# A Trainium2 kernel in detail: the query and key stacks of an eight-wide self attention laid out by DMAs, one per head, in place of 0/1 products and copies from PSUM

## The reference, cut to what matters

```python
q, k, v = x @ Wq, x @ Wk, x @ Wv              # layer 3 also: biases and rotary embedding
q, k, v = (t.reshape(B, T, 16, 8).transpose(0, 2, 1, 3) for t in (q, k, v))
scores = q @ k.swapaxes(-1, -2) / sqrt(8)      # layers 0 and 1: causal
ctx = softmax(scores) @ v                      # T = 512 queries and keys
```

## Time and profile before

| | |
|---|---|
| median of 3 runs | 3211.59 us (3202.09 to 3213.86) |
| profiled execution, its own time | 3200.05 us |
| span in the profile | 3198.3 us |
| PE busy | 2715.7 us (85%) |
| DVE busy | 1759.3 us (55%) |
| ACT busy | 1373.9 us (43%) |
| POOL busy | 602.8 us (19%) |
| mean granted PE clock | 0.87 of full speed |

### The profile page before, as it was taken

How to read it: one execution, slowest core, us unless ns; L and a number is a source line. 1 busy time by engine, 2 the same in 40 slices (tenths; PEclk the granted TensorE clock), 3 DMA queues, 4 the chain that set the end, 5 groups by cost and what they waited for, 6 DMA issues and landing times.

```text
span 3198.3 us, 41256 instructions
## 1 busy us (share of the span) xinstructions
PE 2715.7 (85%) x14161; PEld 1369.0 (43%) x14161; DVE 1759.3 (55%) x4863; ACT 1373.9 (43%) x3204; POOL 602.8 (19%) x849
## 2 busy tenths in 40 slices
PE   6898998889987888888879988987899788889885
PEld 3233335334543675244423333452345347732353
DVE  5535437645654687624565444476357548776154
ACT  2545622452324543564435556225532345335741
POOL 1220001220112672000013200003201138610000
PEclk9988998988878998869779888998898689988776
DMA  4000000000000000000100000000001000000000
GB/s 168 2 1 1 1 1 25 26 2 20 29 19 1 1 27 27 1 1 31 37 8 2 1 1 1 1 26 26 1 20 33 14 1 1 27 28 1 1 1 7
DMA packets 16432, 49.71 MB, mean 16 GB/s; under 512 B 1761, under 2 KB 8801, under 8 KB 14434
## 3 DMA queue, kind: packets, MB, share of 16 engines
q1 hardware_dynamic: 15650, 45.79, 4.1%
q10 hardware_dynamic: 576, 1.29, 0.1%
HBM read 45.43 MB, written 1.05 MB: 15 GB/s over the span
## 4 chain that ended last, share of the span: by engine, by line
PE 66%; DVE 17%; ACT 9%; issue 6%; POOL 1%; DMA 0%; SPq 0%; ACTq 0%; DVEq 0%; POOLq 0%
PE psum L582 5%; PE psum L2155 4%; PE psum L995 4%; PE psum L549 4%; PE psum L572 3%; PE psum L1006 3%; DVE floor_s L2254 2%; PE psum L979 2%; PE psum L1530 2%; PE psum L1822 2%; PE psum L1360 2%; PE psum L821 2%; PE psum L746 2%; ACT PT_s L648 2%; PE psum L1818 2%
## 5 line engine op out<-in xcount | busy, mean ns | idle before, releaser
L648 ACT ACTIVATE PT_s<-psum 128x512 f32<-128x512 f32 (+3 forms) x768 | 344.9, 497 | 277.7 <-PE psum L572 276.0
L396 POOL TENSOR_SCALAR ve<-mv 128x4 f32<-128x4 f32 x48 | 13.5, 281 | 1668.9 <-DVE mv L386 1668.7
L708 DVE CUSTOM_DVE_ANT_0 rest_s<-psum,packed_early 128x128 f32<-128x128 f32 (+3 forms) x512 | 226.6, 487 | 152.2 <-PE psum L555 150.1
L2181 POOL TENSOR_TENSOR buffer<-sim_s 128x1024 f32<-128x1024 f32 x128 | 271.7, 2138 | 171.7 <-DVE floor_s L2254 86.9
L572 PE MATMUL psum<-QS_s,KS_s 64*128 64x512 bf16 (+3 forms) x768 | 199.3, 364 | 36.1 <-DVE mx_s L708 16.6
L555 PE MATMUL psum<-KS_s,QS_s 64*128 64x512 bf16 (+3 forms) x768 | 186.9, 354 | 43.2 <-DVE mx_s L711 20.1
L582 PE MATMUL psum<-PT_s,vaug 128*9 128x512 f32 (+3 forms) x1536 | 179.4, 542 | 45.3 <-POOL PT_s L681 29.4
L681 POOL TENSOR_SCALAR_AFFINE_SELECT PT_s<-PT_s 128x128 f32<-128x128 f32 x512 | 146.0, 294 | 340.3 <-ACT PT_s L648 334.8
L711 DVE TENSOR_REDUCE mx_s<-psum 128x1 f32<-128x512 f32 x256 | 161.8, 683 | 83.7 <-PE psum L555 82.9
L1043 ACT ACTIVATE PT_s<-psum 128x512 f32<-128x512 f32 (+1 forms) x224 | 121.0, 592 | 164.4 <-PE psum L997 164.3
L2214 ACT ACTIVATE above_s<-buffer,below_s 128x1024 f32<-128x1024 f32 x128 | 145.2, 1149 | 96.6 <-POOL buffer L2181 58.0
(11 more groups left out here) (446 smaller groups left out, 5382.8 us busy)
## 6 DMA issues: line engine op xcount, KB each, us to landing
buffer<-packed_experts SPq DMA_DIRECT2D x36, 384.0 KB, 3.3
buffer<-packed_moe SPq DMA_DIRECT2D x4, 2048.0 KB, 8.2
buffer<-packed_cross SPq DMA_DIRECT2D x4, 2048.0 KB, 7.9
buffer<-packed_product SPq DMA_DIRECT2D x4, 1024.0 KB, 4.9
packed_early<-packed_early SPq DMA_DIRECT2D x1, 2654.5 KB
QS_s<-nmT_s SPq DMA_DIRECT2D x144, 4.0 KB
raw_s<-packed_setup SPq DMA_DIRECT2D x1, 1840.0 KB, 7.6
packed_late<-packed_late ACTq DMA_DIRECT2D x4, 314.0 KB, 3.7
```

Of the source, the lines that this page charges most:

```text
L648: a.activation(PT[:, u // 4 % 2, i, q0_of(c):T], bank[u % 3][:, q0_of(c):T], ACT.Exp, scale=scale).then_inc(exp_done.sem, 1)
L708: v.tensor_tensor_reduce(junk[:, u % 2, 0:w], bank[n % 4][:, 0:w], s.w["causal"][:, T - w:T], 1.0, -3e38, ALU.add, ALU.max, mx[:, j, h:h + ...
L2181: g.tensor_tensor(fs[:, n % 2], m[:, 0, :].unsqueeze(2).to_broadcast([P, NK, NK]), m[:, 1, :].unsqueeze(1).to_broadcast([P, NK, NK]), ALU. ...
```

## The change

`parts` now has six slots per operand, in the order of the stack, instead of three. `split_up` writes the three parts to their first slots (`FIRST_SLOT`), and four copies on ACT fill the slots in which a part stands again (`MORE_SLOTS`): for keys and queries each, part one to two more slots, then part two to one more. SP waits for both splits and all four copies and then issues 32 DMAs, one for each head's keys and one for its queries, pair by pair, each from 8 partitions by 6 slots of `parts` to 48 rows of `KS` or `QS`, 1 KB a row. They count on four semaphores (`PAIR_GROUPS`): pair 0; pair 1; pairs 2 and 3; pairs 4 to 7. Two more DMAs bring the rows of ones of `KS` from device memory. The ring holds scores and the one turn alone; before the first score of a group PE waits for the group's DMAs. The stack order within a head becomes row = 6 * d + slot for both operands. `selq`, `selk` and `maxrows` and their loads are gone. Products read the 48 rows (score) or 51 rows (`st`) of a head instead of 64.

```diff
+SLOTS = 6
+FIRST_SLOT = {"q": (0, 3, 5), "k": (0, 1, 2)}
+MORE_SLOTS = {"q": (slice(1, 3), slice(4, 5)), "k": (slice(3, 6, 2), slice(4, 5))}
+PAIR_GROUPS = ((0, 1), (1, 2), (2, 4), (4, 8))
...
-    for i in range(HEADS8 // 2 + 1):
-        if i < HEADS8 // 2:
-            ring += [("stack", 2 * i), ("stack", 2 * i + 1)]
-        if i >= 1:
-            ring += [("score", u) for u in range(2 * TJ * (i - 1), 2 * TJ * i)]
-        if i == HEADS8 // 4 + 1:
+    for i in range(HEADS8 // 2):
+        ring += [("score", u) for u in range(2 * TJ * i, 2 * TJ * (i + 1))]
+        if i == HEADS8 // 4:
             ring.append(("turn", 0))
...
-    parts = s.tile("parts", [P, 2, 3, T], BF16)
+    parts = s.tile("parts", [P, 2, SLOTS, T], BF16)
...
+    def stack(h, more=0):
+
+        return slice(64 * (h % 2), 64 * (h % 2) + SLOTS * HD8 + more)
...
-        pe.wait_ge(*keys_split(4))
-        pe.wait_ge(*queries_split(4))
         pe.wait_ge(*v_ready(1))
...
-            if kind == "stack":
-                i, q = u // 2, 1 - u % 2
-                sel = (s.w["selq"], s.w["selk"])[q]
-                for w in range(3):
-                    mm = pe.matmul(bank[n % 4][:], sel[:, w, i, :], parts[:, q, w, :], start=(w == 0), stop=(w == 2))
-                mm.then_inc(ring_ready.sem, 1)
-            elif kind == "score":
+            if kind == "score":
                 h, j = scores[u]
-                pe.wait_ge(*stacks_copied(2 * (h // 2) + 2))
+                for loaded, (first, last) in zip(pairs_loaded, PAIR_GROUPS):
+                    if u == 2 * TJ * first:
+                        pe.wait_ge(*loaded(64 * (last - first)))
...
     def sync(sp):
+        yield T1 - 2
+        for ready in (keys_split(4), queries_split(4), keys_repeated(2), queries_repeated(2)):
+            sp.wait_ge(*ready)
+        for loaded, (first, last) in zip(pairs_loaded, PAIR_GROUPS):
+            for h in range(2 * first, 2 * last):
+                for q, to in ((1, KS), (0, QS)):
+                    sp.dma_start(to[stack(h), h // 2, :], parts[h * HD8:(h + 1) * HD8, q, :, :]).then_inc(loaded.sem, 16)
+        for o in range(2):
+            row = 64 * o + SLOTS * HD8
+            sp.dma_start(KS[row:row + 3].rearrange("p i t -> p (i t)"), s.ones_rows).then_inc(ones_loaded.sem, 16)
...
+        for n in range(2):
+            for q, name, split, repeated in ((1, "k", keys_split, keys_repeated), (0, "q", queries_split, queries_repeated)):
+                yield T1 - 5 + 2 * n + 0.5 * (1 - q)
+                a.wait_ge(*split(2 * n + 1))
+                to = parts[:, q, MORE_SLOTS[name][n], :]
+                a.copy(to, parts[:, q, FIRST_SLOT[name][n]:FIRST_SLOT[name][n] + 1, :].to_broadcast(to.shape)).then_inc(repeated.sem, 1)
...
-            if kind == "copy":
-                i, q = u // 2, 1 - u % 2
-                n = slot[("stack", u)]
-                a.wait_ge(*ring_ready(counted[("stack", u)]))
-                if q == 1:
-                    a.activation(KS[:, i, :], bank[n % 4][:], ACT.Identity, bias=s.w["maxrows"][:, 0:1]).then_inc(stacks_copied.sem, 1)
-                else:
-                    a.copy(QS[:, i, :], bank[n % 4][:]).then_inc(stacks_copied.sem, 1)
```

More of the change, by code:

```diff
@@ L427, in attention8_plan @@
     ring = []
-    for i in range(HEADS8 // 2 + 1):
-        if i < HEADS8 // 2:
-            ring += [("stack", 2 * i), ("stack", 2 * i + 1)]
-        if i >= 1:
-            ring += [("score", u) for u in range(2 * TJ * (i - 1), 2 * TJ * i)]
-        if i == HEADS8 // 4 + 1:
+    for i in range(HEADS8 // 2):
+        ring += [("score", u) for u in range(2 * TJ * i, 2 * TJ * (i + 1))]
+        if i == HEADS8 // 4:
             ring.append(("turn", 0))
-    follow = {"stack": "copy", "score": "max", "turn": "rows"}
+    follow = {"score": "max", "turn": "rows"}
     for n, (kind, u) in enumerate(ring):
@@ L510, in freed @@
         kind, u = ring[n]
-        if kind == "turn":
-            return max_copied(u + 1)
-        return stacks_copied(u + 1) if kind == "stack" else scores_read(u + 1)
+        return max_copied(u + 1) if kind == "turn" else scores_read(u + 1)
     def tensor(pe):
@@ L657, in split_up @@
     def split_up(eng, q, done):
-        whole, left, part = qk[:, q, :], rest[:, q, :], parts[:, q, :, :]
-        eng.tensor_copy(part[:, 0, :], whole).then_inc(done.sem, 1)
+        whole, left = qk[:, q, :], rest[:, q, :]
+        first, second, third = (parts[:, q, n, :] for n in FIRST_SLOT["qk"[q]])
+        eng.tensor_copy(first, whole).then_inc(done.sem, 1)
         eng.wait_ge(*done(1))
-        eng.tensor_tensor(left, whole, part[:, 0, :], ALU.subtract).then_inc(done.sem, 1)
+        eng.tensor_tensor(left, whole, first, ALU.subtract).then_inc(done.sem, 1)
         yield
         eng.wait_ge(*done(2))
-        eng.tensor_copy(part[:, 1, :], left).then_inc(done.sem, 1)
+        eng.tensor_copy(second, left).then_inc(done.sem, 1)
         eng.wait_ge(*done(3))
-        eng.tensor_tensor(part[:, 2, :], left, part[:, 1, :], ALU.subtract).then_inc(done.sem, 1)
+        eng.tensor_tensor(third, left, second, ALU.subtract).then_inc(done.sem, 1)
     def gpsimd(g_):
```

40 lines of the change are left out of this document (15 added, 25 removed).

## The result

| | before | after |
|---|---|---|
| median | 3211.59 us of 5 (3199.47 to 3213.86) | 3167.63 us of 5 (3166.54 to 3194.17) |
| profiled execution, its own time | 3200.05 us | 3194.17 us |
| mean granted PE clock in the profile | 0.87 | 0.82 |

A forecast was written before the change was run, and what follows sets the result against it. PE was taken to bound the kernel, 66% of its chain. Credits of 113, 20 and 2 us less 12, 24, 4, 9, 4 and 6 made 76, plus 9 for the plan: gain 85, time 3120 us, range 3068 to 3188.

The forecast's parts named there:

- What the change takes away: 576 0/1 products on PE's chain in the rings, 113 us, and the stack copies on ACT, 20 us.
- what is late next: In the rings, DVE and its maxima, close behind PE, take back part of the gain: -9, -4 and -6 us.
- The copies, the plan and the setup: Stack copies gone from ACT, 20 us; shorter planned order, +9 us (-15 to +30); fewer setup loads, +2 us.
- (a): ACT's four new copies and its wait for the split: -12 us, bounds from +6 to -48.
- (b): PE's wait at T1 for split, ACT's last copy, four DMA issues and landing: -24 us, bounds -10 to -45.
- (c): Later pairs' DMAs land in time, barely, for their scores: -4 us, bounds 0 to -25.
- (d): SP's queue: 34 issues ahead of the same run's 12 spreads take 21 us; nothing late, cost 0.
- (e): DMA engines: a run's 1536 rows take 10 us over 8 engines, within SP's 20 us of issue.
- (f): Setup: DVE waited 2.17 us for the last load, of which 1.5 MB go: +2 us.
- The range: Bounds together: gain about 130 us with all good ends, about 20 with all bad; final range 3068 to 3188.
- Rival 2: Something else was as late: first waits, ACT's part and the DVE bound leave 15 to 40 us, 3165 to 3190; 16%.
- Rival 4: SP's issue costs more than 0.63 us: at 0.9 the gain is gone, at 1.1 3220 us or more; 10%.

The follow-up runs named there:

- direct: Changed kernel without its 32 pair DMAs a run; two ACT copies fill pair 0 and all heads read it: 3127.61 us, ratio 0.9747.
- filler6: direct with six idle products ahead of each pair's first score, 576 in all: 3172.31 us, ratio 0.9878.
- one_product: Kernel before, with one 0/1 product per stack instead of three, so 384 of 576 go: 3166.23 us, ratio 0.9859.
- before_wait: Kernel before, plus four DMAs of 24 rows after the split, for which PE waits ahead of its first stack: 3219.05 us, ratio 1.0038.
- direct_rest: Changed kernel with pair 0 filled by two ACT copies, pairs 1 to 7 by their 28 DMAs with all waits: 3136.93 us, ratio 0.9759.
- filler: direct with three idle products ahead of each pair's first score, 288 in all: 3139.57 us, ratio 0.9802.

## Why the prediction had the direction and missed the size

The forecast's direction rested on PE's chain and held. The failed step is the first part of "What the change takes away": 576 products, credited with their 113 us on the chain. Put back as idle products they were worth 42 to 45 us.

- **The products, 113 us.** Measured 45 us (direct to filler6; 42 by the ratios), and 44 for 384 of them in one_product. The forecast took 19 off for what is late next, so 94 stand against 45. The sum took each product's length on the chain as what its removal gives. It isn't: with the products gone the mean granted clock is 0.843 and not 0.871, and 56 us come back in the lengths of three groups of the remaining products (direct against filler6). I had the clock in the earlier trace rows, 0.93 and 0.89 in the two stretches, and asked only how long the products were, never whether the clock would stay.
- **The copies, the plan and the setup, less (a): 20 + 9 + 2 - 12 = 19 us.** From before (3209) to filler6 (3172), which differ in these, it is 37 us, so this side was under by 18. One thing in it the sum had no term for: filler6 reaches its first scores 27 us sooner in all than before (70 against 97), as two copies between tiles of SBUF stand there in place of twelve products and copies from PSUM. The rest can't be told apart further. ACT's four copies took 1048 ns and 624 ns, 39 us in all, where I had 42. ACT waited 33.3 us ahead of them, near the 48 of the bound, but there is no sign that PE stood behind it.
- **(b), 24 us.** 31 to 36, or 33 to 45 by the ratios, and that against direct, which itself has two copies between split and first score. My baseline was another, PE's first stack; for just that wait, in the old order, before_wait has 11 us. And measured to the first score the path became shorter by the change, 97 to 81 us in all, since twelve products and two copies had stood in it before. The first score came 5.3 to 5.8 us after the split in the first four runs and not 4.5: an issue each 0.72 us in place of 0.63, and 3.0 us from the last issue's start in place of 2.65. The wait and its length were right; what it costs at the end depends on the order around it, which the sum of shortfalls doesn't see.
- **(c) and (d), 4 us.** 4 to 9 us by the medians. Groups came late only at pairs 1, 2 and 4 of the first run of all (0.7, 2.9 and 6.0 us of idle), where no other stream's work stands between the scores. SP runs at 0.72 us an issue, 23 us for 32.
- **(e).** The 16 DMA engines were busy 0.40 of 610:650, and no group came late there.
- **(f).** The first split ended 3.0 us earlier than before (36.28 to 39.32): in line with the setup's 2 us.
- **What is late next, 19 us.** In part it came, and at DVE as I had it: PE's idle time ended by the maxima (L708, L711 and their like), over scores, stacks or idle products, and transposed scores, is 60 us in filler6 and 78 in direct. From filler6 to direct idle time rose by 16 in all. Against the kernel before, which has 74, the changed kernel with 72 doesn't wait longer for the maxima; there only the place moved, from stacks and transposed scores to the scores. How much of the 49 us short (94 to 45) is the clock and how much DVE can't be parted, since a score at half clock also hands its bank to DVE later; but 158 us of products left and PE's busy time fell by 58, and that part is no wait for DVE.
- **The range.** By the bounds as listed all good ends together are a gain of 161 us and all bad ends a loss of 33, not "about 130" and "about 20", so the range was narrower than its own terms. And among the terms of what is late next "10.7 left" should be the 12 that the same sentence works out.

In one line: -49 for the products with what is late behind them, +18 for copies, plan and setup, -12 for (b) to (d) make 85 into 42. That these add up to the measured gain is no test of them: they are the steps from before to filler6 to direct to the changed kernel, which add up whatever they are. That the time fell into the range is in part luck, as the second error hid some of the first. Rival 2, "something else was as late", gave the right time, 3165 to 3190, with DVE named for what was more PE's clock. Rival 4's issue cost was 0.72, short of the 0.9 from which it decides. The rule of the Trainium skill's page "DMA: Bandwidth & Descriptors" (section "Bandwidth") against small DMAs is one on the share of the peak rate, measured on loads from device memory that GpSimd issues, and no run here tests it; the fit that the prediction quotes with it stands in that page's section "Anatomy of one DMA — SWDGE (gpsimd) path". The rate is low here, 92 GB/s in 610:650 with all other traffic. What this case shows is that the low rate cost little time, since the later DMAs of a run land while the first pairs are scored: direct_rest pays 9 us (4 by the ratios) for the 336 others, 0.03 us each.

Open: why the pure wait costs 11 us in the old order and three times that in the new one. The clock is not needed for a wait to cost (before_wait, at 0.87), nor a wait for the clock to fall (direct and one_product, which have none); where the wait is put into direct, a third of its price is longer products. And no run sets the clock by itself: that the missing products cost through the clock is read from products, clock and lengths moving together in filler and filler6, back and forth.

## What to carry to other kernels

Before you credit a matmul's length on the critical chain, look at the granted clock of its stretch: where it is near 1.00, ask whether it would stay, and put idle products into the changed kernel to price the removed ones. In a stage ordered by two streams' queues, measure from the last producer to the first consumer; the DMAs took 5.3 to 5.8 us there, products with copies from PSUM 3.5 to 9.3, two direct copies 1.4 to 3.9, and the end moved by nearly as much. Price a DMA's issue from a row of its own shape.

## What was unexpected in the hardware

In the changed kernel the clock fell right behind PE's wait for the first pair (3.7 us idle up to 553.5) and then stayed at 0.50 for 33 us, though PE was busy for 30 of them by the profile:

```profile
546.00:554.00 8.00, 2.67 (x10) 0.74 (x8) 4.98 (x16) 1.91 (x3) 0.00 (x0) 0.99 0.24 34
554.00:587.00 33.00, 30.00 (x109) 17.38 (x109) 28.27 (x113) 6.18 (x12) 2.94 (x1) 0.50 0.25 42
```

direct has no such wait, only gaps (PE busy 4.4 of the 8 us from 521 to 529), and fell at 529 for 31 us. Within them is this stretch, with PE busy all the time and the clock at 0.50 all the same:

```profile
537.00:548.00 11.00, 10.97 (x40) 6.26 (x39) 7.61 (x32) 1.92 (x4) 0.20 (x1) 0.50 0.01 1
```

In the kernel before the clock fell in the same ring, at 552 behind a gap of 1 us, but came back after 7 us; in filler it fell at 546 behind a gap of 1.6 us and came back after 16, with idle products in between. So in these four places the fall follows a gap in PE's work, and what differs is how long the low stretch lasts. The Trainium skill's page "TensorE: Matmul & The Clock Gate" (section "What's actually happening") lets the clock follow how busy PE has recently been. The falls here agree with it, each of the four behind a gap (3.7, 1.6 and 1 us, and 3.6 us in pieces). How long the clock stays low can't be read from the profile's busy share, and one reason is plain: at the lower clock a product lasts longer, so the share goes up without more work being done. A like product over 128x128 f32, in direct at 0.50 (531:559) and in the kernel before at 1.00 (561:589) (xcount, busy us, mean ns):

```profile
L1715 PE MATMUL psum<-buffer,wideT_s 128*128 128x128 f32 x16 | 3.8, 418 | 0.0
```

```profile
L1720 PE MATMUL psum<-buffer,wideT_s 128*128 128x128 f32 x64 | 8.7, 278 | 0.9 <-DVE wideT_s L1756 0.9
```

In the same two windows a product over 128x65 f32 took 429 and 281 ns, a score over 512 columns 611 and 382. What ends a low stretch no run here shows.

A DMA of 8 partitions by 6 slots against 48 rows takes SP 0.67 us and one each 0.72 us, against 0.63 for the spreads' four rows.
